# Mamba state sums shared between VectorE, and ScalarE with accumulating DMAs: a one-core layer on Trainium2

## What is computed

```python
def step(h, inp):
    delta_t, B_t, C_t, x_t = inp
    dA = jnp.exp(delta_t[..., None] * A)
    h = h * dA + (delta_t * x_t)[..., None] * B_t[:, None, :]
    y_t = jnp.einsum('bdn,bn->bd', h, C_t)
    return (h, y_t)
```

## Time and profile before

| | us |
|---|---|
| median of 3 runs | 2025.68 |
| lowest, highest | 2025.44, 2032.33 |
| the profiled execution | 2031.67 |
| its span, first to last instruction | 2029.9 |
| TensorE, busy | 1695.2 |
| VectorE, busy | 1528.3 |
| GpSimd, busy | 993.6 |
| ScalarE, busy | 793.0 |
| starts of the four blocks (c_now copied) | 123.5, 392.9, 673.9, 952.8 |

### The profile page before, as it was taken

How to read it: one execution, slowest core, us unless ns; L and a number is a source line. 1 busy time by engine, 2 the same in 40 slices (tenths; PEclk the granted TensorE clock), 3 DMA queues, 4 the chain that set the end, 5 groups by cost and what they waited for, 6 DMA issues and landing times. The chain is left out here.

```text
span 2029.9 us, 28313 instructions
## 1 busy us (share of the span) xinstructions
PE 1695.2 (84%) x7908; PEld 1258.7 (62%) x7908; DVE 1528.3 (75%) x2037; ACT 793.0 (39%) x1162; POOL 993.6 (49%) x767
## 2 busy tenths in 40 slices
PE   3856777597888888887867779889989999999998
PEld 2344444464445654445444454777878999999997
DVE  0379999999999999999999970477735566556564
ACT  0455555455465465564554431100002233323232
POOL 0067558676478585586776844000004444343343
PEclk9967888699898799897988879899999999999999
DMA  4212211122213222213222243211115666665664
GB/s 101 65 43 59 63 45 48 59 80 79 69 52 104 69 80 86 60 53 110 67 67 64 58 148 112 101 63 62 66 52 128 163 152 140 168 156 136 162 172 66
DMA packets 131939, 184.18 MB, mean 91 GB/s; under 512 B 23313, under 2 KB 81441, under 8 KB 128609
## 3 DMA queue, kind: packets, MB, share of 16 engines
q1 hardware_dynamic: 109200, 132.52, 20.2%
q0 software_dynamic: 17856, 44.85, 11.3%
q10 hardware_dynamic: 4720, 4.86, 0.9%
HBM read 277.64 MB, written 38.15 MB: 156 GB/s over the span
## 5 line engine op out<-in xcount | busy, mean ns | idle before, releaser
L1017 POOL TENSOR_TENSOR arena_kept<-arena_kept,b_all 128x512 f32<-128x512 f32 x512 | 642.0, 1279 | 313.5 <-DVE arena_kept L912 297.5
L912 DVE TENSOR_TENSOR_SCAN arena_kept<-da,arena_kept 128x512 f32<-128x512 f32 x512 | 596.5, 1205 | 19.8 <-ACT da L790 19.8
L790 ACT ACTIVATE da<-arena_kept,a_neg 128x504 f32<-128x504 f32 x512 | 348.5, 685 | 423.5 <-DVE arena_kept L912 419.9
L590 PE MATMUL hT<-ident_kept,arena_kept 128*128 128x128 f32 x2048 | 321.7, 316 | 188.7 <-DVE arena_kept L912 188.2
L590 PEld LDWEIGHTS hT<-ident_kept,arena_kept 128*128 128x128 f32 x2048 | 282.8, 165 | 282.6 <-DVE arena_kept L912 245.5
L925 DVE SCALAR_TENSOR_TENSOR yacc<-hT,c_now,yacc 128x512 f32<-128x512 f32 x480 | 332.7, 734 | 5.5 <-PE hT L590 4.3
L443 PE MATMUL bank<-hid,wt 128*128 128x512 f32 x512 | 259.5, 657 | 26.4 <-ACT arena_kept L646 25.7
L1912 POOL DMA_INDIRECT out<-y,slots_kept x76 | 132.0, 1737 | 258.1 <-issue 186.8
L443 PEld LDWEIGHTS bank<-hid,wt 128*128 128x128 f32 x512 | 104.6, 214 | 142.0 <-issue 113.7
L830 DVE SCALAR_TENSOR_TENSOR arena_kept<-xpad,ch,arena_kept 128x512 f32<-128x512 f32 x96 | 78.5, 817 | 64.5 <-ACT arena_kept L646 62.2
L1780 ACT ACTIVATE gs<-egp 128x352 f32<-128x352 f32 x73 | 33.8, 463 | 235.8 <-PE eup L1112 227.4
(11 more groups left out here) (214 smaller groups left out, 3110.3 us busy)
## 6 DMA issues: line engine op xcount, KB each, us to landing
w_up_kept<-in_up_T SPq DMA_DIRECT2D x76, 1408.0 KB, 6.1
w_dn_kept<-in_dn_T SPq DMA_DIRECT2D x76, 768.0 KB, 7.4
b_all<-bt_scratch SPq DMA_DIRECT2D x128, 256.0 KB, 3.5
wt<-in_in_T SPq DMA_DIRECT2D x64, 256.0 KB, 3.0
wt<-in_out_T SPq DMA_DIRECT2D x32, 256.0 KB, 2.9
x_in<-in_x_pad ACTq DMA_DIRECT2D x16, 256.0 KB
res<-in_x_pad SPq DMA_DIRECT2D x16, 256.0 KB, 4.5
x_scratch<-res SPq DMA_DIRECT2D x16, 256.0 KB, 2.0
```

Source lines behind the costliest of these rows:

```text
L590: mm = nc.tensor.transpose(hT[t][:, d * P:(d + 1) * P], h[:, m % RING, d, t * P:(t + 1) * P], ident[:])
L790: nc.scalar.activation(out[:, :, 1:], rows[:, :, 1:], ACT.Exp, scale=a_neg[:, d, n:n + 1]) \
L912: nc.vector.tensor_tensor_scan(h[:, n % RING, i, :], da[i % RING][:], dbx[:, i, :], 0.0, ALU.mult, ALU.add).then_inc(scan_done, 1)
L1017: nc.gpsimd.tensor_tensor(dbx[:, i, :], u[:, d, :], b_all[:, m % RING, :], ALU.mult) \
```

## The change

For tiles 2 and 3 (`SHIFTED`) and the first 14 states of each half (`SHIFTED_STATES`), VectorE no longer adds the state. Two steps later ScalarE reads hT[t] from PSUM times c_now (`scale_state`), for tile 2 behind decay 1 and for tile 3 behind decay 2. For the first state of a half it writes straight into yacc[t], for the others into a buffer `stage` with one slot per tile. GpSimd then issues, behind the 4 inflows of the step and ahead of its gate and delta pieces, a DMA that adds stage to yacc in SBUF (`add_shifted`). ScalarE may overwrite the slot when all earlier adds of that tile have landed (`added`). States 14 and 15 of these tiles, and tiles 0 and 1, stay on VectorE. TensorE waits for `scaled` in place of sum_done where the state before was shifted. To make room for `stage`, xam moves into the second slot of x2_sb (with a wait for its stores), and the weight slots go from 6 to 5. The semaphore counts of sum_done are worked out by a function, and scan 0 of a step now waits for the transposes of two steps back.

```diff
+SHIFTED = (2, 3)
+SHIFTED_STATES = NST - 2
+
+def shifted(m, t):
+    return t in SHIFTED and m % NST < SHIFTED_STATES
+
+def sums_by_dve(j, m, t):
+    own = [(k, tile) for k in range(STEPS) for tile in range(TB) if not shifted(k, tile)]
+    return j * len(own) + sum(at <= (m, t) for at in own)
+
+def scaled_by_act(j, m):
+    return j * HALVES * SHIFTED_STATES + m // NST * SHIFTED_STATES + min(m % NST + 1, SHIFTED_STATES)
+
+def added_states(j, m):
+    return scaled_by_act(j, m) - (j * HALVES + m // NST + 1)
...
-SLOTS = 6
+SLOTS = 5
...
-    xam = sb("xam", [NADAPT * LRANK, BLK])
+    xam = x2_sb[:, 1, :]
+    stage = sb("stage", [P, len(SHIFTED), HT * P])
...
             def turn(at, half):
-                pe.wait_ge(sum_done, at.block * SUMS + SUM0 + (0 if half else SUMS // HALVES))
+                pe.wait_ge(sum_done, sums_by_dve(at.block - 1, STEPS - 1, TB - 1) if half else sums_by_dve(at.block, NST - 1, TB - 1))
...
             def turn_h(j, m, tiles):
                 pe.wait_ge(scan_done, j * SCANS + SCAN0 + HT * (m + 1))
+                last = (j, m - 1) if m else (j - 1, STEPS - 1)
                 for t in tiles:
-                    pe.wait_ge(sum_done, j * SUMS + TB * m + t + 1)
+                    if last[0] >= 0 and shifted(last[1], t):
+                        pe.wait_ge(scaled[t], scaled_by_act(*last))
+                    elif last[0] >= 0:
+                        pe.wait_ge(sum_done, sums_by_dve(*last, t))
...
+            def scale_state(j, m, t):
+                n = m % NST
+                act.wait_ge(hT_full, j * SUMS + TB * m + t + 1)
+                if n == 0:
+                    act.wait_ge(c_copied, j + 1)
+                    if m or j:
+                        act.wait_ge(bank_full, Place("body", j, "turn0" if m else "turn1").uses[-1].number + 1)
+                    out = yacc[:, t, :]
+                else:
+                    act.wait_ge(added[t], ADDED * (added_states(j, m) - 1))
+                    out = stage[:, SHIFTED.index(t), :]
+                nc.scalar.mul(out, hT[t][:], c_now[:, t, n:n + 1]).then_inc(scaled[t], 1)
...
                         decay(j, *divmod(m, NST), i)
+                        for t in SHIFTED:
+                            if m >= 2 and shifted(m - 2, t) and i == t - SHIFTED[0] + 1:
+                                scale_state(j, m - 2, t)
...
             def masked(at):
+                dve.wait_ge(x2_stored[1], 16 * TB // RING * b)
...
             def scan(j, g, n, i):
+                if i == 0 and j * SUMS + TB * (m - 1) > 0:
+                    dve.wait_ge(hT_full, j * SUMS + TB * (m - 1))
...
             def add_state(j, g, n, t):
+                m = g * NST + n
+                if shifted(m, t):
+                    return
...
-                    dve.wait_ge(sum_done, at + SUM0 - TB + 1)
+                    if shifted(m - 1, t):
+                        dve.wait_ge(added[t], ADDED * added_states(j, m - 1))
+                    else:
+                        dve.wait_ge(sum_done, sums_by_dve(j, m - 1, t))
...
             for j in range(NBLK):
                 dve.wait_ge(dve_emptied, turned_bc(j).dve + 1)
-                dve.wait_ge(sum_done, j * SUMS + SUM0)
+                if j:
+                    dve.wait_ge(sum_done, sums_by_dve(j - 1, STEPS - 1, TB - 1))
+                    for t in SHIFTED:
+                        dve.wait_ge(scaled[t], scaled_by_act(j - 1, STEPS - 1))
...
+            def add_shifted(j, m, t):
+                pool.wait_ge(scaled[t], scaled_by_act(j, m))
+                nc.gpsimd.dma_start(out=yacc[:, t, :], in_=stage[:, SHIFTED.index(t), :], accum_op=ALU.add) \
+                    .then_inc(added[t], ADDED)
...
                 for m in range(STEPS):
                     for i in range(HT):
                         inflow(j, *divmod(m, NST), i)
+                    for t in SHIFTED:
+                        if m >= 2 and (m - 2) % NST and shifted(m - 2, t):
+                            add_shifted(j, m - 2, t)
```

More of the change, by code:

```diff
@@ L297, in mamba @@
     sum_done = sem("sum_done")
+    scaled = {t: sem(f"scaled{t}") for t in SHIFTED}
+    added = {t: sem(f"state_added{t}") for t in SHIFTED}
     c_copied = sem("c_copied")
     y_ready = [sem(f"y_ready{half}") for half in range(HALVES)]
-    DBX0, SCAN0, SUM0 = RING * HT, HT, TB
+    DBX0, SCAN0 = RING * HT, HT
+    ADDED = 16
     SKIP0, Y0 = 1, HT
@@ L535, in mixed @@
                 pe.wait_ge(dve_emptied, Place(section, j, "xa").dve + 1)
-                nc.tensor.matmul(bank[:], b_T[:, e * P:(e + 1) * P], xam[:], start=False, stop=True).then_inc(bank_full, 1)
+                nc.tensor.matmul(bank[:], b_T[:, e * P:(e + 1) * P], xam, start=False, stop=True).then_inc(bank_full, 1)
             def x2_row(section, j, at, t):
@@ L869, in masked @@
                 dve.wait_ge(mask_step, 2)
+                dve.wait_ge(x2_stored[1], 16 * TB // RING * b)
                 dve.wait_ge(bank_full, at.full + 1)
-                nc.vector.tensor_tensor(xam[:].rearrange("p (b l) -> p b l", b=BB), banks[at.bank][:].rearrange("p (b l) -> p b l", b=BB),
+                nc.vector.tensor_tensor(xam.rearrange("p (b l) -> p b l", b=BB), banks[at.bank][:].rearrange("p (b l) -> p b l", b=BB),
                                         mask[:, b * BB:(b + 1) * BB].unsqueeze(2).broadcast_to([P, BB, SEQ]),
@@ L915, in add_state @@
             def add_state(j, g, n, t):
-                at = j * SUMS + TB * (g * NST + n) + t
+                m = g * NST + n
+                if shifted(m, t):
+                    return
                 scalar = c_now[:, t, n:n + 1]
-                dve.wait_ge(hT_full, at + 1)
+                dve.wait_ge(hT_full, j * SUMS + TB * m + t + 1)
                 if n == 0:
@@ L928, in _ @@
             dve.sem_inc(scan_done, SCAN0)
-            dve.sem_inc(sum_done, SUM0)
             for s in range(RING):
```

## The result

The changed kernel takes 2131.91 us (median, 2130.1 to 2134.14) against 2028.14 for the kernel before: the ratio is 1.0506, with a 95% interval of 1.0491 to 1.0522. It is 5% slower, where 4% faster was forecast. The profiled execution took 2133.26 us.

The account below looks back on a forecast made before the run. VectorE was taken to bound the four blocks (1083 us of the span). Removed sums 146 us less give-backs of 60 leave 86: 2025.7 to 1940 us, or 1910 to 1975 with give-backs 30 to 95; overall range 1895 to 2005.

Parts of the forecast that it names:

- What goes: VectorE in the four blocks: 224 sums, or 112 pairs at 1.30 us, go; 146 us, the most possible.
- give-backs: Time lost again to ScalarE 30, GpSimd 13, denser GpSimd 5, TensorE 22 us: 70, counted as 60 for overlap.
- ScalarE: 224 scaled copies from PSUM at 687 ns behind decays 1 and 2; mostly covered, 30 us given back.
- Silu steps: Steps with a four-tile Silu and two table loads, 4.47 us on ScalarE: 14 at 1.8 us, 25 us.
- GpSimd's issues: 208 add issues at 1.0 us; GpSimd 240 us a block, over VectorE's 233 in block 0; 13 us charged.
- in a bare step that suffices: GpSimd waits for the tile-3 copy; time until the same slot's next scan covers it in a step with nothing else.
- The port: Denser GpSimd meets VectorE instructions with two SBUF inputs: 5 us; 96 us by the whole-instruction blocking rule, set aside.
- The ring: Copy m waits until add m-1 lands, 4.9 us from issue; hides within a step, cost 0.
- The rival on the slower side: ScalarE's wait for landed adds ahead of the tile-3 copy sets the step; at 9.5 us landing 2150 us; chance 0.11.
- TensorE: Loses no work but must fit shorter steps, nearly full in out-projection steps: 22 us given back.
- GpSimd becomes the bound: An add issue costs 1.59 us, GpSimd 271 us in blocks 0 to 2: 1985 to 2010 us; chance 0.15.
- GpSimd over 0.97 busy: Sign of the case where GpSimd binds, along with scans waiting for its inflows (L1017).

Follow-up runs that it names:

- e2: Changed kernel with ScalarE's scaled copies but without the add DMAs: 1977.95 us.
- e3b: Changed kernel with the 208 transfers as plain copies issued by ScalarE, none by GpSimd, ScalarE still waiting for their landing: 1983.54 us.
- e4: Changed kernel with the adds turned into plain copies, still issued by GpSimd: 2092.2 us.
- e1_floor: Changed kernel without the copies and without the adds, the shifted sums simply left out: 1951.2 us beside 2027.8 for the kernel before.
- e14_early: Changed kernel with VectorE's taps, corrections and products moved from behind scan 3 to behind the sums after scan 1, one step later: 2092.48 us.
- e5: Changed kernel without VectorE's 32 corrections (rounding term of the softplus): 2099.47 us.
- e17_lag3_early: Changed kernel with adds a step later (four stage slots, three weight slots, half the shifted states left out) and VectorE's pieces behind scan 1: 2092.99 us.

## Why the prediction was wrong

The chain of runs gives the balance: without the sums -77 us; copies +27 (e2); plain transfers with the wait for landing +6 (e3b), which single executions can't tell from nothing; the same issued by GpSimd +109 (e4); accumulating +40. The sum is +105 by rounding, for the 104 measured. It has to come out, as each term is one run less the one before it; what the runs add is which step costs what, for this order of steps.

**What goes: mis-sized.** 146 us was called the most that the change can give; 77 is. The spacing of 1.30 us a pair was right: VectorE is 113 us less busy in e1_floor with 30 us of hold added, so 143 us of sums left it. But the shortened step ran closer to GpSimd's and TensorE's work at once, and 69 us came back before any copy or add was made. The give-backs were listed under the added work, 60 us in all, while the removal alone brought more than that.

**ScalarE: right in size.** 675 ns a copy for 687 forecast, and 27 us for the copies where 30 was charged. How much of the 27 is the Silu steps, which the 30 were charged for, and how much TensorE's waits for the copies is not shown.

**GpSimd's issues: the price was right, its place wrong.** An issue took 1.04 us in the median (mean 1150 ns) for the 1.0 taken, and a block of GpSimd 236 us for the 240 forecast (the last is in part luck, as rows of issues and inflows overlap and the inflows grew). The step that failed is the charge of 13 us by comparing busy sums of a block. "Just under" VectorE's time is no cover when the two engines feed each other slot by slot: GpSimd must wait for scans and for copies (100 and 127 us) and can't make up a lost microsecond. The sentence "in a bare step that suffices" looked at the next inflow's deadline; what it missed is the run of four unbroken inflows that comes of a late start. In place of the 13 us, moving plain transfers from ScalarE's queue to GpSimd's cost 109 us, with the hold in it, and accumulating 40 more.

**The port: the term that was furthest off.** Charged 5 us; the three groups rose by 126 us of VectorE's busy time. The prediction had the rule before it and the size that it would give, 96 us, and set it aside because the taps averaged 817 ns with GpSimd at 0.68. That average was taken where GpSimd runs in short pieces with gaps. The Trainium skill (SBUF — State Buffer, Summary: rules for kernel authors) says that, where VectorE's instruction has two SBUF inputs and GpSimd's reads SBUF, the second one to issue blocks fully until the first finishes. The trace agrees that it is held, and for longer than that: one correction took 4.89 us, until four inflows were over. But the port is not the sole cause: freeing it gave 39 us (e14_early) or 32 (e5), and then the scans waited for GpSimd.

**The ring: right.** Forecast at 4.9 us from issue to landing, measured 4.9 (3.2 to 9.1), and a longer ring won nothing. The rival on the slower side (the ring) had the sign of the result for the wrong reason, and at its price of 2150 us only looked close. The Trainium skill's fit for such a DMA (DMA: Bandwidth & Descriptors, Anatomy of one DMA) gives an estimate of 2.6 us for 256 KB issued by GpSimd. The runs differ from it: plain transfers from GpSimd landed in 3.7 us in the median, accumulating ones in 4.9; plain ones issued by ScalarE in 2.8. DMA share was 0.45 to 0.51, not 0.7: the adds took less of the DMA engines than the rows of the scatter suggested.

**TensorE:** the prediction said that it loses nothing, but its transposes now wait 162.9 us for ScalarE's copies, and its clock did not rise: 0.78, 0.87, 0.86 and 0.79 granted for 0.79, 0.88, 0.88 and 0.85 before. Of the 22 us charged to it, the runs show only the 27 us that VectorE waits for its transposes in e1_floor.

**The rivals.** "GpSimd becomes the bound" named the engine and gave 1985 to 2010. It could not reach over 2028, because it again took the longer of two busy sums. The signs that would prove it, "GpSimd over 0.97 busy", did not come: it is at 0.78, as in the one-tile kernel that gains. Other signs came true and said nothing: 288 sums are left, and the scans idle 64 us more for the 60 forecast. But of these, waits for decays are only 14 us (33.8 for 19.8); waits for inflows, 37.5 us where there were none, are the largest part.

What stays open: how much of the remaining 60 us in e17_lag3_early is the issues' length and how much their place within GpSimd's list; a kernel with accumulating issues and no other work of GpSimd was not tried. Nor is it shown why merged adds a step later lose more than in place: the wait for landing is longer (304.8 us for 217.9), and GpSimd also waits 104.2 us for b_all, where it was 6.0 in place.

## What to carry to other kernels

When two engines hand slots to each other, price an instruction added to either by what it delays in the other's order, not by the sum of busy times. A first look at that is cheap: move the same work to another queue, as e3b did. And before making one engine denser, list the instructions of its neighbour that read two inputs from SBUF; a mean taken while GpSimd had gaps says nothing of what they cost when it has none. Where a shift overshoots, half of it may be the optimum (here one tile of four, 0.36% faster).

## What was not expected of the hardware

A VectorE instruction with two SBUF inputs can be held through several GpSimd instructions in a row, not just the one that runs when it arrives: 4.89 us beside four inflows that together take 5.57, and a median of 4.1 us over the 32 corrections. It isn't always held: in e1_floor 12 corrections took 0.67 to 0.69 us, though the next inflow began within 0.1 us of their start. What decides between the two is not shown. An accumulating issue takes GpSimd nearly twice a plain one (medians of 1.04 and 0.57 us, both 256 KB), and one of 512 KB no longer than one of 256 KB (0.88 against 1.04 us). Accumulating transfers also keep the DMA engines busy for longer than plain ones of the same size and number: a share of 0.49 of the blocks against 0.36 in e4_pool_plain, and 0.24 before.
